# A gated cross- and self-attention layer with experts on one core: the self-attention's value products in two groups of 64 keys

## The reference, cut to what matters

```python
h = rmsnorm(x, ln1_w)
q = (h @ wq).reshape(b, s, H, HD)
k = (h @ wk).reshape(b, s, H, HD)
v = (h @ wv).reshape(b, s, H, HD)
scores = jnp.einsum('bqhd,bkhd->bhqk', q, k) / np.sqrt(HD).astype(np.float32)
causal = jnp.tril(jnp.ones((s, s), bool))
scores = jnp.where(causal, scores, jnp.float32(-1000000000.0))
attn = jax.nn.softmax(scores, axis=-1)
ao = jnp.einsum('bhqk,bkhd->bqhd', attn, v).reshape(b, s, H * HD) @ wo
```

## Time and profile before

| | |
|---|---|
| median of three runs | 696.73 us |
| profiled execution | 695.13 us |
| its span, first to last instruction | 693.3 us |
| instructions in the span | 14660 |
| granted TensorE clock, mean | 0.998 |
| moved by DMA | 50.08 MB |

### The profile page before, as it was taken

The page is one execution under the profiler, slowest core; times in us unless marked ns, Lnnn a source line. Parts: engine busy times, 40 slices in busy tenths (PEclk is TensorE's granted clock), DMA queues, the critical chain, the costliest instruction groups (busy, mean ns, idle before and its releaser), DMA issues.

```text
span 693.3 us, 14660 instructions
## 1 busy us (share of the span) xinstructions
PE 673.0 (97%) x5422; PEld 586.7 (85%) x5422; DVE 458.9 (66%) x881; ACT 341.6 (49%) x688; POOL 304.0 (44%) x372
## 2 busy tenths in 40 slices
PE   8799999999899999999999999999999999999997
PEld 6588878888787898999889889998888888888886
DVE  4567777769666666676665758865555888655555
ACT  4567667567665334524344523345446644444443
POOL 4534433534333243433333335334554566655553
PEclk9999999999999999999999999999999999999999
DMA  6511221110101123221212212111332332333332
GB/s 204 164 60 46 60 80 48 36 35 25 35 12 32 46 69 99 63 77 61 62 61 90 78 62 62 46 32 46 97 98 80 92 92 77 105 92 91 91 92 91
DMA packets 35850, 50.08 MB, mean 72 GB/s; under 512 B 4048, under 2 KB 22864, under 8 KB 35792
## 3 DMA queue, kind: packets, MB, share of 16 engines
q1 hardware_dynamic: 35504, 49.03, 23.6%
q10 hardware_dynamic: 288, 0.26, 0.1%
HBM read 48.22 MB, written 1.05 MB: 71 GB/s over the span
## 4 chain that ended last, share of the span: by engine, by line
PE 85%; DVE 6%; ACT 4%; POOL 3%; issue 2%; DMA 0%; SPq 0%; DVEq 0%; POOLq 0%; ACTq 0%
PE acc L539 20%; PE bank_k L512 15%; PE bank_q L512 14%; PE bank_v L613 7%; PE bank_v L512 5%; PE bank_s L659 5%; PE bank_s L512 4%; PE bank_p L680 2%; PE bank_p L645 2%; PE bank_q L634 2%; POOL sq_k_lo L1455 2%; PE bank_p L690 2%; PE bank_t L690 2%; PE bank_t L667 2%; ACT sq_q L901 1%
## 5 line engine op out<-in xcount | busy, mean ns | idle before, releaser
L539 PE MATMUL acc<-wo_hi,pv_hi 128*128 128x256 f32 x328 | 94.6, 288 | 2.1 <-DVE pv_lo L1325 1.5
L1455 POOL TENSOR_TENSOR sq_k_lo<-sq_k,sq_k_hi 128x512 fp32r<-128x512 f32 x32 | 48.6, 1518 | 102.7 <-ACT sq_k_hi L910 102.7
L539 PE MATMUL acc<-wo_lo,pv_hi 128*128 128x256 f32 x328 | 92.6, 282 | 0.0
L539 PE MATMUL acc<-wo_hi,pv_lo 128*128 128x256 f32 x328 | 92.2, 281 | 0.0
L1455 POOL TENSOR_TENSOR wq_lo<-raw_m,wq_hi 128x256 fp32r<-128x256 f32 x50 | 44.1, 883 | 59.9 <-DVE wq_hi L1283 55.7
L906 ACT ACTIVATE kt<-bank_k 128x512 f32<-128x512 f32 x64 | 38.3, 598 | 64.0 <-PE bank_k L512 64.0
L539 PEld LDWEIGHTS acc<-wo_hi,pv_hi 128*128 128x128 f32 x328 | 61.5, 188 | 6.4 <-DVE pv_lo L1325 2.4
L539 PEld LDWEIGHTS acc<-wo_lo,pv_hi 128*128 128x128 f32 x328 | 61.8, 188 | 1.8
L539 PEld LDWEIGHTS acc<-wo_hi,pv_lo 128*128 128x128 f32 x328 | 62.0, 189 | 0.0
L984 ACT ACTIVATE pv_hi<-rows_t 128x512 fp32r<-128x512 f32 x50 | 31.6, 632 | 61.2 <-DVE rows_t L1321 59.5
L1325 DVE TENSOR_TENSOR pv_lo<-rows_t,pv_hi 128x512 fp32r<-128x512 f32 x50 | 37.1, 743 | 36.0 <-ACT pv_hi L984 36.0
(11 more groups left out here) (202 smaller groups left out, 1981.5 us busy)
## 6 DMA issues: line engine op xcount, KB each, us to landing
raw_m<-in_chunk_m SPq DMA_DIRECT2D x50, 256.0 KB, 2.7
raw_a<-in_head_a SPq DMA_DIRECT2D x48, 192.0 KB, 2.5
raw_b<-in_head_b SPq DMA_DIRECT2D x32, 256.0 KB, 2.9
raw_m<-in_chunk_m SPq DMA_DIRECT2D x50, 128.0 KB, 2.1
raw_v<-in_pair_v SPq DMA_DIRECT2D x16, 256.0 KB, 2.8
raw_b<-in_head_b SPq DMA_DIRECT2D x32, 128.0 KB, 2.2
out<-xs SPq DMA_DIRECT2D x4, 256.0 KB, 2.3
xs<-in_x SPq DMA_DIRECT2D x6, 128.0 KB, 3.0
```

The source lines that it names most:

```text
L539: last = nc.tensor.matmul(acc[t // 2][:, (t % 2) * D:(t % 2 + 1) * D], w[:, tok], m, start=begins and n == 0, stop=True, skip_group_check= ...
L1455: nc.gpsimd.tensor_tensor(lo, raw, hi, ALU.subtract).then_inc(signal, 1)
```

## The change

The turned weights are copied as they are, by one ACT instruction, into `rows_t`; `attn_t`, its memset and one semaphore go. Since the two 64-row halves of `rows_t` hold the keys of two sequences, `head_values` takes 16 products of 64 rows instead of 8 of 128: for each of the 8 groups (2 heads by 4) one from the lower and one from the upper half of the partitions, 128 weight columns and 64 moving columns each. The results are collected by half, not by head: lower half in bank_p, upper half in bank_t, both heads in each. There is one semaphore increment for the whole block, so both ACT copies come after it; they and DVE's subtractions write `pv_hi` and `pv_lo` in runs of 64. Output of either head now waits for both subtractions. The two `raw_a1` buffers become slices of one, whose first 512 columns `hh` uses in the experts' stage.

```diff
-    SETUP = 8
+    SETUP = 7
...
-        raw_a1 = [sb(f"raw_a1_{p}", [P, A1]) for p in range(2)]
+        raw_a = sb("raw_a", [P, 2 * A1])
+        raw_a1 = [raw_a[:, p * A1:(p + 1) * A1] for p in range(2)]
...
-        attn_t = sb("attn_t", [P, G, SPB, SEQ])
...
-        hh = rows_t[:].rearrange("p n h q -> p (n h q)")
+        hh = raw_a[:, 0:HT]
...
+        def by_sequence(ap, row):
+
+            return ap.rearrange("p h (n r q) -> p h n r q", r=SPB, q=SEQ)[:, :, :, row, :]
...
-                    pe.wait_ge(B["pv_lo"], u.of(h))
+                    pe.wait_ge(B["pv_lo"], u.of(1))
...
-            def head_values(u, h):
+            def head_values(u):
 
                 pe.wait_ge(B["vs"], 2 * u.n)
-                pe.wait_ge(B["attn_t_lo"], u.n)
                 pe.wait_ge(B["attn_t"], u.n)
-                for n in range(NT):
-                    last = nc.tensor.matmul(value_bank(h)[:, n * P:(n + 1) * P], vs[:, n, h * P:(h + 1) * P],
-                                            attn_t[:, h * NT + n, :, :], start=True, stop=True)
+                turned = rows_t[:].rearrange("p n h q -> p (n h q)")
+                for g in range(G):
+                    h, n = divmod(g, NT)
+                    cols = slice(g * SEQ, (g + 1) * SEQ)
+                    for r in range(SPB):
+                        rows = slice(r * SEQ, (r + 1) * SEQ)
+                        last = nc.tensor.matmul(value_bank(r)[:, cols], vs[rows, n, h * P:(h + 1) * P], turned[rows, cols],
+                                                start=True, stop=True)
                 last.then_inc(B["pv_done"], 1)
...
-                    act_e.wait_ge(B["pv_done"], u.of(1) - 2)
+                    act_e.wait_ge(B["pv_done"], u.n - 1)
...
-                for r, signal in ((0, B["attn_t_lo"]), (1, B["attn_t"])):
-                    rows = slice(r * SEQ, (r + 1) * SEQ)
-                    nc.scalar.activation(attn_t[rows, :, r, :], groups(bank_t[rows, :]), ACT.Copy).then_inc(signal, 1)
+                nc.scalar.activation(rows_t[:].rearrange("p n h q -> p (n h q)"), bank_t[:], ACT.Copy).then_inc(B["attn_t"], 1)
...
-            def take_head_values(u, h):
-                act_e.wait_ge(B["pv_done"], u.of(h))
-                nc.scalar.activation(pv_hi[:, h], value_bank(h)[:], ACT.Copy).then_inc(B["pv_hi"], 1)
+            def take_head_values(u):
+                act_e.wait_ge(B["pv_done"], u.n)
+                for r in range(SPB):
+                    nc.scalar.activation(by_sequence(pv_hi[:], r), by_tile(value_bank(r)[:]), ACT.Copy).then_inc(B["pv_hi"], 1)
...
-            def split_head_values(u, h):
-                v.wait_ge(B["pv_hi"], u.of(h))
-                nc.vector.tensor_tensor(pv_lo[:, h], value_bank(h)[:], pv_hi[:, h], ALU.subtract).then_inc(B["pv_lo"], 1)
+            def split_head_values(u):
+                for r in range(SPB):
+                    v.wait_ge(B["pv_hi"], u.of(r))
+                    nc.vector.tensor_tensor(by_sequence(pv_lo[:], r), by_tile(value_bank(r)[:]), by_sequence(pv_hi[:], r),
+                                            ALU.subtract).then_inc(B["pv_lo"], 1)
...
-            nc.gpsimd.memset(attn_t[:], 0.0).then_inc(setup_pool, 1)
```

More of the change, by code:

```diff
@@ L326, in flamingo_layer @@
         B = stage_sems("b", "wq_hi wq_lo wk_hi wk_lo wv_hi wv_lo wo_hi wo_lo q_done k_done v_done qt kt vs scores scaled "
-                       "max sub exp sum inv norm t_done attn_t_lo attn_t pv_done pv_hi pv_lo wo_done")
+                       "max sub exp sum inv norm t_done attn_t pv_done pv_hi pv_lo wo_done")
         M = stage_sems("m", "wg_hi wg_lo wu_hi wu_lo wd_hi wd_lo g_done u_done silu weighted hh hh_hi hh_lo down")
@@ L398, in load_a1 @@
             def load_a1(u, h):
-                sp.dma_start(raw_a1[h][:], head_a[2 * u.i + h, :, 0:A1]).then_inc(ld_a1[h], 16)
+                sp.dma_start(raw_a1[h], head_a[2 * u.i + h, :, 0:A1]).then_inc(ld_a1[h], 16)
             def load_a2(u, h):
@@ L798, in self_pair @@
                 release(held[:1])
-                for h in range(2):
-                    head_values(u, h)
+                head_values(u)
                 if nxt.kind == "b":
@@ L1036, in self_pair @@
                 prepare(u, 1)
-                for h in range(2):
-                    take_head_values(u, h)
+                take_head_values(u)
                 if nxt.kind == "b":
@@ L1397, in self_pair @@
                     multiply_up(nxt)
-                for h in range(2):
-                    split_head_values(u, h)
+                split_head_values(u)
                 if nxt.kind == "b":
```

## The result

The changed kernel took 707.18 us in the median of 4 runs (705.05 to 709.14), beside 697.31 us (695.54 to 698.38, 4 runs) of the kernel before on the same chip: ratio 1.014, 95% interval 1.0116 to 1.0165. Timed once more, apart from these runs (e9), it gave 707.65 against 698.69 us, ratio 1.0121, 1.0097 to 1.0144. So the change costs 9 to 10 us; 9.8 were forecast. Single executions of one kernel differ by up to 5 us. The profiled execution took 707.14 us, with a span of 705.4 us.

The account below looks back on a forecast made before the run. PE, busy 97% of the span, was taken to bound the kernel. 15 x (0.34 + 0.33) - 0.5 + 0.2 = +9.8 us on 696.73 us gives 706.5 us; range 700.5 to 710.

Parts of the forecast that it names:

- The block: Head-value products on PE: 16 steps of 0.110 us plus 0.28 entry and exit, 2.04 us against 1.70, +0.34 a pair.
- ACT's order: ACT's value copy now behind two result copies delays PE's second value projection, 1.48 to 1.81 us: +0.33 a pair.
- The logits pair: Head values there waited for ACT's second copy of turned weights; one copy instead of two saves 0.5 us.
- The 15 pairs: Pairs followed by another self-attention pair: each grows by 0.34 for the block and 0.33 for the wait.
- The last pair: Products can start a little earlier, but output waits for the second pv_lo: +0.2 us, between 0 and +0.34.
- Costs put at nothing: Copies and subtractions in runs of 64 keep their price; later key copy, pv_lo and weight splits cost nothing.
- The start: Removing attn_t's memset (0.95 us on POOL) lets PE's warm-up start sooner, without gain: 0, -0.3 to +0.3 us.
- A: Rival, chance 0.13: the head-value step halves with the moving columns to 0.056 us; -3.6 us, 693.1 us.
- C: Rival, chance 0.04: a group's load and product don't overlap when the product is short; another 13.6 us, 720 us.
- E: Rival, chance 0.02: a head-value step between 0.063 and 0.080 us, so that gains and wait cancel within 0.3%.
- B: Rival, chance 0.08: ACT's queue hides the third copy behind the head values; +4.8 us, 701.5 us.
- D: Rival, chance 0.01: the row groups don't run side by side, 32 steps of 0.107 us a block; over 730 us.

Follow-up runs that it names:

- e9: The changed kernel itself, unaltered, timed once more beside e10: 707.65 us against 698.69 for the kernel before, ratio 1.0121.
- e1: The changed kernel with a spare memset of 128x1024 at the place of the removed one: median 704.18 us of 6 runs.
- e10: The changed kernel with the spare memset, the same file as e1, timed again beside the changed kernel itself: 706.16 us.
- e2: The changed kernel with ACT's copy of the next values ahead of its two result copies: median 701.04 us, ratio to the kernel before 1.0051.
- e6: The kernel before with ACT's copy of the next values between the two result copies: median 695.59 us against 697.41, ratio 0.9971.
- e3: The changed kernel with 32 instead of 64 moving columns in each head-value product, half of the queries left out: 705.54 us, one execution.
- e4: The changed kernel with 64 instead of 128 weight columns in each head-value product, half of the value columns left out: 693.26 us, one execution.
- e5: The kernel before with attn_t's memset last on POOL and PE's warm-up not waiting for it: 697.83 us against 697.41, ratio 1.0002.
- e7: The changed kernel with e2's order and each head-value product split into two column groups of 64 weight columns: median 688.05 us, ratio to the kernel before 0.9864.
- e11: The kernel of e7 with 25 instead of 20 warm-up products and e8's filling: median 685.97 us, ratio to the kernel before 0.9831.
- e8: The kernel before with 8 products over zeros in PE's first wait for squares of the keys: median 695.25 us against 697.41, ratio 0.9972.

## Why the prediction was right

Forecast 706.5 us and +9.8 us; measured 707.18 and, in two measurements, +9.9 and +9.0. The mechanism was right in both of its terms. That +9.9 falls within 0.1 us of the forecast is partly luck: from the first head values on the profiles differ by 8.8 us, and the rest comes with the start, in which executions of the same kernel differ by more than that (e1 and e10, one and the same file: first head values at 244.46 and 249.29 us). By its steps:

- **The block.** Forecast +0.34 us a pair from a step of 0.110 and 0.28 us of entry and exit. Measured a step of 0.111, 2.02 us for the block where 2.04 were forecast, so +0.32 (+0.36 by the difference of e2 and e6); entry and exit come to 2.02 - 16 x 0.111 = 0.24. That the step follows the weight columns, which rested on the 16-column logits and on the differences between load records, is shown by e3 and e4.
- **ACT's order.** Forecast: the projection's first load 1.81 us after PE's next block instead of 1.48, +0.33. Measured 1.81. The start of the value copy, forecast 1.11 us after that block, was 1.09. My "just met" was too kind to the kernel before: this order already cost it 0.08 us a pair in the rows of e6 and up to 0.12 in the whole pair, 1.2 to 1.8 us in all, which e2 took back as well.
- **The logits pair.** Forecast -0.5 from ACT's single copy; the interval from that pair's predecessor fell from 17.46 to 17.36 us, though it holds one more +0.64, so -0.74: the term was mis-sized by a quarter of a microsecond, to the good side.
- **The 15 pairs.** Forecast 0.67 each. Of the 15 intervals between blocks of head values, 12 grew by 0.61 to 0.69 us, one by 0.51, that of the logits pair fell by 0.10, and the last grew by 0.48 only. That these two ordinary intervals would grow less was not foreseen.
- **The last pair.** Forecast +0.2. From its head values to the end of the span it was 223.18 us and is 223.32, +0.14. As forecast, output waits for the second pv_lo, which shows in PE's timeline and answers to the earlier trace rows:

```profile
486.10 0.39 PE L543 MATMUL acc<-wo_hi,pv_hi 128*128 128x256 f32 x1 [0.43 <-DVE pv_lo L1218]
```

- **Costs put at nothing.** ACT's copies in runs of 64 take 592 to 597 ns and DVE's subtractions 681 and 692 ns, as before. Scores and the weights' splits caused no new wait.
- **The start.** Forecast 0, -0.3 to +0.3. The profiles differ by 3.35 us there, far outside; e5, e7 and e10 put most of this down to differences between executions, and the 1.5 us between e9 and e10 are left open for the memset. So the runs do not show that this term was mis-sized, but its margin was too small for comparing two single profiles. Of the profiles' 12.1 us, 8.61 lie between the first and the last head values, 0.14 behind, 3.35 ahead; the forecast for the first two together was 9.8 and they measured 8.75, 1.0 less.
- **The range.** By its own terms (a step of 0.107, a wait of 0.15) the lower end of the forecast's own range is 703.0 and not 703.5 us; nothing hangs on it.

Rivals A, C and E were excluded by the step of 0.111 in the changed kernel, and A's mechanism by e3; B by the wait that e2 removes; D by the two groups' common starts.

## What to carry to other kernels

Splitting a product in two row groups halves its rows and its moving columns and doubles the records, which then run two at a time. That gained nothing here: as long as every record still comes with a load of 128 float32 weight columns, it takes 0.11 us in its group, whether 128, 64 or 32 columns move, and the entry and exit of the form come on top. Halving the weight columns too, and using the column groups for the other half, did gain: together with the value copy moved ahead on ACT it turned +1.4% into -1.4% (the move alone led to +0.5%). And before merging two releases into one, look at what stands in the reader's queue behind the copies, above all where that wait is only just met already. If the copy goes ahead of them, look at what meets PE next: here it was the softmax on DVE, in two pairs.

## What the runs showed of the hardware that I had not expected

Four groups of 64x64 kept a record starting every 0.059/4 = 0.015 us on average, 64 records in 1.10 us from the first to the next block. I had held a cost of some 0.027 us a record for possible, and no row gives that figure: the 32 records of the scores block take 1.08 us in the chain, 0.034 each. The Trainium skill's page "TensorEngine Tiling (Array Packing)" says under its key properties that tiles load and multiply independently; this trace agrees.

The kernel before itself runs between 694.8 and 700.4 us over all its executions. Over the profiles of all forms the granted clock in the start goes along with where the first head values fall. With 26 to 30 us at 1.00 behind 0.53 to 0.55 in 23 to 26 us they come at 244.5 to 244.8 us (before, e1, e7). With 0.50 in 23 to 26 us and 0.50 to 0.86 in 26 to 30 us they come at 246.2 to 249.3 us, in forms with and without the memset. In e11, at 1.00 throughout 12 to 30 us, they come at 243.5 us. In e8, where the low clock came at 32 us, it was 245.9 us. That the two go together is read off 13 profiles; only e8 and e11 changed the idle time on purpose.
